# Moving three instructions inside one step of an attention pipeline: masked low part, second half of the projection, weight squares

## The reference

```
q = rmsnorm(rope(h @ Wq_c @ Wq_up));  k = rmsnorm(rope(h @ Wk));  v = h @ Wv
ck = rmsnorm(blocks of 16 tokens of h @ W_comp)
c_out  = softmax over [q.ck * scale for finished blocks, sink] @ ck
sw_out = softmax over [50 * tanh(q.k * scale / 50) for the last 128 keys, sink] @ v
x = x + ga * (((c_out + sw_out) @ Wg) @ Wo)
```

## Time and profile before

| what | value |
|---|---|
| median of 3 runs | 984.08 us (982.18 to 984.67) |
| the profiled execution | 984.83 us, its span 983.1 us |
| granted clock of TensorE, mean | 0.974 |
| busy over the span | PE 92%, PEld 78%, DVE 69%, ACT 59%, POOL 57% |
| attention, 230 to 436 us | PE 204.5, DVE 188.3, POOL 185.0, PEld 175.1, ACT 164.2 us busy |

### The profile page before, as it was taken

One profiled execution on the slowest core, in us unless ns is written; L12 is line 12 of the kernel. 1 busy time (PEld: TensorE's weight loads), 2 busy tenths in 40 slices (PEclk: granted clock), 3 DMA queues, 4 the chain that ended last, 5 costly groups with the idle time before them and its releaser, 6 DMA issues. The chain is left out here.

```text
span 983.1 us, 16741 instructions
## 1 busy us (share of the span) xinstructions
PE 908.0 (92%) x5022; PEld 768.9 (78%) x5022; DVE 680.8 (69%) x1256; ACT 575.9 (59%) x1565; POOL 563.7 (57%) x759
## 2 busy tenths in 40 slices
PE   4988999789999999998899999999859899999996
PEld 4987776568888888887788888888748688888885
DVE  3464569589989999999989989999747433332312
ACT  0454454567887877777778788787434523324221
POOL 0055200668899888888889888888323323232222
PEclk9998899889999999999999999999979999999999
DMA  8566668113224142141241422422071020020101
GB/s 278 179 203 237 229 219 279 51 31 126 68 79 140 52 142 78 55 155 37 78 140 57 137 79 68 149 83 75 12 301 41 1 86 1 1 86 0 44 1 45
DMA packets 68725, 101.29 MB, mean 103 GB/s; under 512 B 16176, under 2 KB 48432, under 8 KB 65712
## 3 DMA queue, kind: packets, MB, share of 16 engines
q1 hardware_dynamic: 56528, 72.65, 23.1%
q10 hardware_dynamic: 12128, 27.71, 7.8%
HBM read 82.64 MB, written 26.35 MB: 111 GB/s over the span
## 5 line engine op out<-in xcount | busy, mean ns | idle before, releaser
L1055 PE MATMUL banks<-fold,aoT 128*128 128x512 f32 x768 | 194.8, 403 | 2.2 <-DVE aoT L1277 2.2
L1858 POOL TENSOR_TENSOR gus<-arena,gus 128x512 fp32r<-128x512 f32 x43 | 65.0, 1512 | 183.3 <-ACT gus L1760 183.3
L1055 PEld LDWEIGHTS banks<-fold,aoT 128*128 128x128 f32 x768 | 140.7, 190 | 30.6 <-DVE aoT L1277 2.5
L1824 DVE SCALAR_TENSOR_TENSOR arena<-banks,sg,arena 128x512 f32<-128x512 f32 x44 | 33.1, 751 | 133.4 <-ACT arena L1755 133.4
L1055 PE MATMUL banks<-k_st,qT 128*128 128x256 f32 x768 | 108.2, 291 | 0.0
L1755 ACT ACTIVATE arena<-banks,sg 128x512 f32<-128x512 f32 x44 | 30.4, 691 | 124.9 <-PE banks L1714 124.9
L1714 PE MATMUL banks<-hT_even,w_hi 128*128 128x512 f32 x352 | 87.0, 399 | 12.5 <-issue 9.7
L1055 PEld LDWEIGHTS banks<-k_st,qT 128*128 128x128 f32 x768 | 96.4, 191 | 0.4 <-DVE qT L1322 0.4
L1678 PE MATMUL banks<-w_hi,gus 128*128 128x512 f32 x352 | 87.2, 390 | 1.9 <-DVE gus L1829 1.1
L1430 POOL TENSOR_TENSOR pp<-pp,kons 64x512 fp32r<-64x512 f32 x64 | 85.6, 1338 | 5.0 <-ACT pp L1193 5.0
L1714 PEld LDWEIGHTS banks<-hT_even,w_hi 128*128 128x128 f32 x352 | 66.4, 192 | 28.0 <-issue 10.1
(11 more groups left out here) (198 smaller groups left out, 2151.7 us busy)
## 6 DMA issues: line engine op xcount, KB each, us to landing
arena<-in_wq_blocks ACTq DMA_DIRECT2D x8, 1056.0 KB, 4.9
wq_words<-in_wq_blocks ACTq DMA_DIRECT2D x8, 1056.0 KB, 6.9
w_lo<-wq_words SPq DMA_DIRECT2D x11, 768.0 KB, 9.2
go_raw<-in_w_go SPq DMA_DIRECT2D x16, 512.0 KB, 5.6
k_st<-k_parts SPq DMA_DIRECT2D x32, 192.0 KB, 2.8
arena<-in_L_attn_h SPq DMA_DIRECT2D x32, 128.0 KB, 2.9
comp_raw<-in_w_comp SPq DMA_DIRECT2D x16, 256.0 KB, 3.9
v_st<-v_parts SPq DMA_DIRECT2D x32, 128.0 KB, 2.1
```

Source lines behind the costliest of these rows:

```text
L1055: last = pe.matmul(out, lhs[a], rhs[b], start=start and q == 0 and u == 0, stop=stop and q == n - 1 and u == 2)
L1824: dve.scalar_tensor_tensor(gu[:, n % 2], GU[2 * (n % 2) + 1][:], sg[:, 1, h:h + 1], gu[:, n % 2], ALU.mult, ALU.mult).then_inc(gued, 1)
L1858: pool.tensor_tensor(gus[:, n % 2, 1], gu[:, n % 2], gus[:, n % 2, 0].bitcast(F32), ALU.subtract).then_inc(gu_lo, 1)
```

## The change

The order of three lists is changed, and nothing else. On PE, `project_second` moves from behind `project_first` to between `window_values` and `compressed_values`. On ACT, `weight_squares` moves from behind `probs_high` to behind `exp`, and `over_sum` goes ahead of `compressed_exp`. On DVE, `masked_low` moves from behind `merge` to right behind `probs_low`.

```diff
         steps(pe, (0, query), (3, transpose_probs), (2, scores), (3, transpose_compressed), (4, project_first),
-              (4, project_second), (1, transpose_query), (3, window_values), (3, compressed_values), alone=EVERY,
+              (1, transpose_query), (3, window_values), (4, project_second), (3, compressed_values), alone=EVERY,
               after={2: first_transposes})
...
-        steps(act, (4, out_high), (3, probs_high), (0, weight_squares), (0, squares), (3, compressed_high), (2, tanh), (2, exp),
-              (1, query_high), (2, compressed_exp), (2, over_sum), after={3: first_channels})
+        steps(act, (4, out_high), (3, probs_high), (0, squares), (3, compressed_high), (2, tanh), (2, exp), (0, weight_squares),
+              (1, query_high), (2, over_sum), (2, compressed_exp), after={3: first_channels})
...
-        steps(dve, (4, out_low), (5, tile_out), (3, probs_low), (2, compressed_logits), (2, merge), (3, masked_low),
+        steps(dve, (4, out_low), (5, tile_out), (3, probs_low), (3, masked_low), (2, compressed_logits), (2, merge),
               (3, compressed_low), (2, compressed_max), (2, window_sum), (0, scale_query), (1, query_low), (2, compressed_sum),
```

## The result

The changed kernel takes 998.94 us (median of 4 runs, 996.09 to 1001.5) against 983.13 us before (median of 4): a ratio of 1.0166, 95% interval 1.0118 to 1.0215. It is slower, as forecast; 993 us had been forecast, so the loss is 15.8 us where 8.9 were forecast. The profiled execution took 1001.41 us, its span is 999.6 us against 983.1: 16.5 us more. From the first to the last end of DVE's masked product are 527.0 us against 509.5, so the whole loss, 17.5 us, lies in the attention; the rest of the kernel, whose code is the same, took 1.0 us less.

A forecast was written before the change was run, and what follows sets the result against it. PE, 0.2 to 0.4 us a step short of its 7.61 us floor through a loop via DVE. Early steps +7.8, late +3.8 and -2.7, together 8.9 us on 984.8, gave 993.7, stated as 993; range 970 to 1004.

The forecast's parts named there:

- The floor and the loop: Attention step: PE's work is 7.61 us, missed by 0.2 to 0.4 us through a loop via DVE, with L1316's 1.37 us in it.
- the race: Whether DVE's masked product (L1316) or POOL's (L1430) starts first; the other waits for its end.
- The half projection: On PE: `window_values` wants to start 4.47 us after `query`, not 5.88, and needs POOL's masked product; 3.14 us later comes `query`.
- The masked product: On DVE: ready 2.70 us after `query`, not 3.62, but waits for L1467's end and needs 0.54 us more.
- The rival in which L1467 holds nothing up: DVE's masked product no longer waits for POOL; steps fall to PE's 7.61 us, 17 us faster, 967 us; chance 0.12.
- POOL keeps the pair: Waiting DVE isn't let in before POOL's next product; 0.9 us a step, +50 us, 1034 us; chance 0.07.
- The sum: Attention steps won and lost by turns: 8.30 us late and 8.10 early, against 8.03 and 7.82; together 8.9 us more.
- M: The end of DVE's masked product in a step, from which the prediction counts its times.
- The rival in which DVE wins everywhere: DVE's masked product goes first in every step; every step is 7.84 us, -5 us, 979 us; chance 0.17.
- the term that took half of the late steps as won: Late attention steps: 14 at 7.84 us against 8.03, -2.7 us, because the first late race is lost by only 0.07 us.
- all late steps lost: Variant within the forecast's spread of 988 to 1001: 28 late steps at 0.27 us more each, 999 us.
- the signs: Expected in the profile: tanh waiting for merge, L1338 for `compressed_exp`, PE for L1430, and L1316 in two kinds by turns.

## Why the prediction was right or wrong

*The floor and the loop.* That PE had about 0.3 us a step in hand, and that DVE's masked product with its wait for POOL was what kept it from them, is shown by the kernels with DVE's move and without PE's: 7.7 us a step, close to PE's 7.61. But the loop that set the step before is not the one that the prediction named, through PE's transposes, the high part and `query`. In that kernel L1316 ended after L1430, and L1430 came from DVE's sum L1338 by way of POOL (L1338 starts 3.27 us after the masked product's end, L1467 ends at 6.10, L1430 starts at 6.06). The run with PE's move alone starts `query` 0.46 us later and leaves this loop at 7.9. The sum did follow POOL's chain, so the forecast did not suffer. Nor does the growth of L1285 lengthen every step of the late half: ordinary steps have 7.9 us in both halves. What differs is the step with `add_tile`, every fourth. In the early half DVE wins the race in it, and it takes 7.1 or 7.2 us and the next one 8.3. In the late half L1285 has grown and DVE loses by 0.01 to 0.11; it takes 8.3 or 8.4 and the next one 7.9.

*The half projection.* The prediction had `window_values` meet L1430's end at 4.47 us of the step with nothing in hand. Shown: it waits (0.63 us in the step above), and putting it back alone gives 28 us.

*The masked product.* DVE is held up by L1467 as well: 0.54 after its end in the step above. The rival in which L1467 holds nothing up is out. So is the one in which POOL keeps the pair: DVE came in between two POOL instructions that stand back to back. The Trainium skill (SBUF — State Buffer, Who interferes with whom) has the blocking and its order of issue so, and the runs agree (0.54 us after L1467's end); that the waiting engine gets in between two instructions of the other is told by the runs alone.

*The sum.* After a won race it had DVE ready at M + 7.15 and L1430 issued at M + 7.08; measured from M = 394.34 they are 7.22 and 7.17. Wins and losses by turns, 7.67 and 8.92 forecast late in a sequence, are 7.7 to 7.9 and 8.9 to 9.0. The rival in which DVE wins everywhere did not come about in the changed kernel, where L1430 was first in 28 steps.

*The step that failed* is the term that took half of the late steps as won. It rested on 0.07 us, "no more than my semaphores are sure to", and hardly any was won out of turn: two in each sequence. The rows say why. In a late step with no other work DVE comes at M + 7.14, as reckoned, and L1430 at 7.11 to 7.19 as its tile grows: that is one race lost by 0.03 and then two won by 0.02 and 0.05. But the sum left out two things that come every fourth step. `tile_out` (L1363) lies on DVE ahead of L1303: in the step above ACT's high part ended at 400.72, L1303 started only at 400.84, and L1316 came at M + 7.22, 0.08 later than without it, in a race that was lost by 0.05. Three late races of each sequence go this way. `add_tile` lies on POOL. In every second step that has it, DVE's product runs ahead of L1467 too; POOL's masked product then ends 1.84 us after DVE's, `query` comes at M + 5.16, and DVE loses the next race by 0.6 to 0.7 us. No run took `tile_out` or `add_tile` away; this is read from the trace of the changed kernel.

With all late steps lost the text gave 999, and the median is 998.94. That they agree so closely is luck: the profiled execution took 1001.41, and smaller terms were off both ways. Early steps were to have 8.10 and had 8.22. The compressed scores start 0.04 us behind the masked product (394.34 to 394.38), not 0.08 ahead of its end, and what stands behind them is later by 0.08 in the step above (L1338 at M + 4.37, reckoned 4.29); besides, L1285 takes 0.22 to 0.33 us in the early half, and the sum had 0.22 for all of it. Late steps with the races by turns were to have 8.30 and had 8.25, with the two that were won out of turn. Times 28 that is 3 us more and 1.4 us less. Why DVE doesn't overlap these two instructions stays open.

Of the signs, tanh waits for merge as foretold. DVE's L1338 waits for `compressed_exp` only 3 times in the stretch (1.1 us in all), and no wait of PE in the list names L1430.

*ACT's moves* were costed at nothing beyond the lateness of L1338, which was counted. Without them 13.5 of the 17.5 us remain, so they do carry some 4. The weight squares cost nothing: with them DVE's move has 504.1 us of attention, without them 506.7.

## What to carry to other kernels

A move that shortens one engine's path can take away the distance that kept another pair of waits apart: here one of two good-looking moves gave 0.4% alone and the other cost 0.7%, and only together did they set up a race that was lost in nearly every second step, for 1.7%. Where two engines take turns at something exclusive, look at who is issued first and by how much; in this kernel a margin of hundredths of a microsecond decided over more than a whole one. Making the order certain was worth 9 us of the changed kernel, but it matters for whom: with POOL always first the best order of the other lists lost 5 us. Look also for work that comes only every few steps: it decides such a race even where its own time costs nothing. Before believing a delay experiment, read in its trace that the delay has moved the instruction it was meant to move.

## What the runs showed of the hardware

An instruction of DVE with two operands in SBUF that is issued in the midst of a POOL instruction of the same kind gets in when that ends, ahead of the next POOL instruction in the queue, even where that one is issued 0.04 us before the end; it then ends 0.54 us after the release. The POOL instruction behind it (1.30 us by itself) ends 1.15 to 1.16 us after DVE's (395.49 less 394.34, and at 246 us).

POOL's memsets, which read nothing from SBUF, did not hold DVE's product up: it took 0.68 us beside them, at 416.91.

That added work on one engine makes a kernel 9 us faster I had expected from the sum, but not that the order which makes ACT's chain longer would be a good companion of DVE's move: 968.6 us, 1.35% below the kernel before. Three more kernels lie so close to it (970.6, 969.5 and 969.0 us; 498.4, 499.7 and 497.9 of attention against its 499.5) that none of the four can be called the fastest.
